# In L0's head pipeline, the product of the next gated input moves to the end of TensorE's sixth slot, and ScalarE copies it first in the seventh

## What is computed

```python
a  = tanh(einsum('ble,hde->blhd', emb, Wa_w) + Wa_b)
bg = einsum('ble,hde->blhd', emb, Wb_w) + Wb_b
h  = at * h + bt                       # scan over the tokens, for each of 8 heads
Dx = emb @ D_w.T + D_b                 # the "gated input": one for all heads
out = (einsum('blhd,hkd->blhk', hs, C_w) + C_b) * Dx[:, :, None, :]
out = _ln(out, hn_g, hn_b)
sum_heads = (Dx + einsum('h,blhd->bld', head_w, out)) / nH
z = sum_heads @ Wout_w.T + Wout_b
u = z + _ln(z, norm_g, norm_b)
ffn = gelu(u @ ffn1_w.T + ffn1_b)
return (u + (ffn @ ffn2_w.T + ffn2_b)) @ proj_w.T + proj_b
```

## Time and profile before

| | us |
|---|---|
| median of 3 runs | 1346.33 |
| lowest, highest | 1341.58, 1354.73 |
| the profiled execution | 1357.45 |
| its span | 1355.7 |
| L0's layer in it, from the first scan to the last tile's end | about 343 to 716 |

### The profile page before, as it was taken

One profiled execution on the slowest core, in us unless ns is written; L12 is line 12 of the kernel. 1 busy time (PEld: TensorE's weight loads), 2 busy tenths in 40 slices (PEclk: granted clock), 3 DMA queues, 4 the chain that ended last, 5 costly groups with the idle time before them and its releaser, 6 DMA issues.

```text
span 1355.7 us, 17322 instructions
## 1 busy us (share of the span) xinstructions
PE 1125.2 (83%) x4988; PEld 819.3 (60%) x4988; DVE 889.2 (66%) x2544; ACT 700.8 (52%) x1314; POOL 618.1 (46%) x725
## 2 busy tenths in 40 slices
PE   5866999992888999999966668999983678898996
PEld 4655877871565667666735456888861445555563
DVE  7746788773786777777727436777772377776661
ACT  4223767771456656666532214777752335554532
POOL 5864000005687888777625744000016466664440
PEclk9658999996899999999975657999995688888997
DMA  7536467751000000000000104477731000000000
GB/s 240 188 131 215 164 227 221 244 165 51 20 15 13 12 15 12 13 5 1 1 1 18 47 30 143 162 243 245 242 131 43 16 16 16 24 24 12 8 9 23
DMA packets 48958, 115.43 MB, mean 85 GB/s; under 512 B 8160, under 2 KB 14304, under 8 KB 48864
## 3 DMA queue, kind: packets, MB, share of 16 engines
q1 hardware_dynamic: 40672, 97.53, 22.0%
q0 software_dynamic: 8192, 16.79, 4.2%
HBM read 79.16 MB, written 35.13 MB: 84 GB/s over the span
## 4 chain that ended last, share of the span: by engine, by line
PE 54%; POOL 14%; DVE 12%; issue 9%; ACT 6%; another core or an unknown queue 3%; DMA 1%; SPq 0%; POOLq 0%; DVEq 0%; ACTq 0%
PE bank L188 6%; PE bank L331 4%; PE bank L333 4%; PE bank L332 4%; PE bank L345 3%; PE bank L344 3%; PE bank L343 3%; PE bank L890 2%; PE bank L1384 2%; POOL head_rstd L1101 2%; PE bank L1405 2%; PE bank L930 2%; POOL wr L488 2%; PE bank L936 2%
## 5 line engine op out<-in xcount | busy, mean ns | idle before, releaser
L609 DVE TENSOR_TENSOR hid_lo<-hid,hid_hi 128x512 fp32r<-128x512 f32 x248 | 170.3, 689 | 101.5 <-ACT hid L411 91.5
L458 POOL DMA_INDIRECT xs<-spare_all,slots x128 | 131.9, 1031 | 72.2 <-issue 37.7
L488 POOL DMA_INDIRECT got<-ys,y_slots x64 | 67.2, 1050 | 197.5 <-DMA ys<-spare_all 183.5
L411 ACT ACTIVATE hid<-bank,b_up_of 128x512 f32<-128x512 f32 x184 | 125.5, 682 | 6.2
L188 PEld LDWEIGHTS bank<-ident,spare_all 128*128 128x128 f32 x568 | 78.0, 156 | 71.6 <-issue 63.3
L410 ACT ACTIVATE hid_hi<-bank,b_up_of 128x512 fp32r<-128x512 f32 x138 | 95.0, 689 | 45.0 <-PE bank L333 34.2
L188 PE MATMUL bank<-ident,spare_all 128*128 128x128 f32 x568 | 93.9, 297 | 20.5 <-DVE spare_all L518 13.1
L984 ACT ACTIVATE gate_b<-bank,head_rstd 128x128 f32<-128x128 f32 x256 | 72.8, 369 | 49.7 <-POOL head_rstd L1101 49.5
L410 ACT ACTIVATE hid_hi<-bank,cols_sb 128x512 fp32r<-128x512 f32 x48 | 33.1, 689 | 117.4 <-PE bank L333 50.2
L331 PE MATMUL bank<-xh,wr 128*128 128x512 f32 x184 | 81.0, 440 | 0.3 <-DVE xl L602 0.2
L1555 POOL MEMSET wz<- 128x128 f32 x1 | 0.2, 204 | 175.0 <-DVEq L678 175.0
(11 more groups left out here) (284 smaller groups left out, 3114.7 us busy)
## 6 DMA issues: line engine op xcount, KB each, us to landing
wr<-wq SPq DMA_DIRECT2D x92, 512.0 KB, 4.4
spare_all<-xs SPq DMA_DIRECT2D x46, 256.0 KB, 4.8
ys<-spare_all SPq DMA_DIRECT2D x46, 256.0 KB, 5.0
wq<-wr SPq DMA_DIRECT2D x16, 512.0 KB
got<-in_w_mlp SPq DMA_DIRECT2D x9, 512.0 KB
xs<-X SPq DMA_DIRECT2D x16, 256.0 KB
xs<-spare_all,slots POOLq DMA_INDIRECT x128
out_x<-X SPq DMA_DIRECT2D x8, 256.0 KB, 2.3
```

The source lines that it names most:

```text
L411: nc.scalar.activation(hid[:, n % HC], bank[n % 3][:], ACT.Gelu_apprx_tanh, bias=bias).then_inc(s["gelu_done"], 1)
L458: g.indirect_dma_start(out=xs, out_offset=bass.IndirectOffsetOnAxis(ap=slots[:, k, n:n + 1], axis=0), in_=xn_all[:, n], in_offset=None).th ...
L488: nc.gpsimd.indirect_dma_start(out=rows_of(i, ring)[:, k, b], out_offset=None, in_=ys, in_offset=bass.IndirectOffsetOnAxis(ap=y_slots[:, k ...
L609: v.tensor_tensor(hid_lo[:, q], hid[:, n % HC], hid_hi[:, q].bitcast(F32), ALU.subtract).then_inc(s["lo_done"], 1)
```

## The change

PE's `dx_of(tile+1)` moves from between `project_head` and `c_of_head` of slot 6 to near the end of slot 5: in slot 5 it stands after `project_head`, `c_of_head`, `turn_head` and `out_of_head`. ACT's `keep_dx(tile+1)` stays in slot 6, but stands first there, ahead of `keep_head` and `share_head`; it stood behind both. Nothing is added or taken away, and all waits inside the functions stay as they are.

```diff
@@ mix_pe @@
                 if n < HEADS:
                     project_head(n)
-                if phase == DX and n // NH + 1 < TILES:
-                    dx_of(tile + 1)
                 if 0 <= n - 1 < HEADS:
                     c_of_head(n - 1)
@@
                 if phase == TURN_U and before_it is not None:
                     turn_u(before_it)
+                if phase == DX - 1 and n // NH + 1 < TILES:
+                    dx_of(tile + 1)
                 if phase == NH - 1 and before_it is not None:
                     up(before_it, 0)
@@ mix_act @@
                 tile, before_it, two_before = mix_tiles(n)
+                if phase == DX and n // NH + 1 < TILES:
+                    keep_dx(tile + 1)
                 if n < HEADS:
                     keep_head(n)
@@
                 if phase == UN and before_it is not None:
                     normalize_z(before_it)
-                if phase == DX and n // NH + 1 < TILES:
-                    keep_dx(tile + 1)
```

## The result

The changed kernel is faster. The medians of six runs each are 1328.1 us and 1350.0 us, and the ratio is 0.985 (95% interval 0.981 to 0.989). The prediction was 1332.5 us with a range of 1326 to 1341. It was counted from 1346.33 us, the median of the first three of the six runs before.

A forecast was written before the change was run, and what follows sets the result against it. PE nearly sets the pace, losing 14.5 us waiting for ACT's Dx copy. Shorter waits (9.4 us) and two thirds of 6.6 us of clock (4.4) make 13.8 us: 1346.33 to 1332.5 us, range 1326 to 1341.

The forecast's parts named there:

- The wait and its reason: Tiles 1 to 6, slot 6: PE waited 14.5 us for ACT's Dx copy, queued behind scalings awaiting POOL's root.
- The moved product: PE's next Dx product, three matmuls of 0.69 us in all, moved to slot 5: no wait added, priced at nothing.
- The moved copy: ACT's Dx copy at the front of slot 6: 0.57 us, hidden by 0.51 us of waiting for POOL.
- What ends the waits next: Slots 6 and 7: u (line 1215), then head 4's statistics (line 1167) release PE; 9.4 us gained over six tiles.
- The clock: Slot 7 of tiles 1 to 4: slow stretches of 1.64 us each go, up to 6.6 us; 4.4 us counted.
- rival 1: PE's wait goes, but slow stretches stay or turn up elsewhere: 1336.9 us, or 1340.2 at its far end; chance 0.26.
- The start: Tiles 0 and 1: PE's product could wait about 0.1 us for line 1157; put at nothing.
- The sum: Whole kernel: 9.4 us of waits and 4.4 us of clock, 13.8 us off 1346.33, giving 1332.5 us; chance 0.48.

The follow-up runs named there:

- The doubled copy: Changed kernel with one more, unread ACT copy of bank 6 at the front of slot 6: L0 306.85 us, ratio 0.990 to the kernel before.
- the filler: Kernel before with eight unused matmuls ahead of turn_u in slot 6 of tiles 1 to 6: L0 312.66 us against 319.03, ratio 0.996.
- the repetition: Changed kernel run once more, unchanged, against the kernel before: medians 1293.1 and 1307.8 us, ratio 0.989, L0 304.67 us.
- the kernel that holds PE: Changed kernel, but PE waits ahead of turn_u in tiles 1 to 6 for ACT's scalings of head 3: L0 312.35 us, ratio 0.995.
- the last kernel: Changed kernel with u normalized ahead of the scalings in tiles 1 to 5 and ACT's old order in tile 0: L0 301.42 us, ratio 0.987.

## Why the prediction was right, step by step

- **The wait and its reason.** Right. Only the copy's place behind POOL's root held PE; the copy alone moved gives the whole gain, and holding PE without touching ACT's order takes half of it back.
- **The moved product.** It was priced at nothing, and it is nothing. What the prediction did not say, though its rows held it, is that this half of the change does no work: the product was done at 497.7 with ACT free at 498.4.
- **The moved copy.** Right: 0.57 us, hidden by the 0.51 us of waiting for POOL. The doubled copy shows the price without the cover, 0.3 us a tile.
- **What ends the waits next.** Right: line 1215 and then line 1167. They were to hold PE for 0.4 us each; the view has 0.2 us of idle time for each, and by the distance of the starts (lines 890 to 188, 1.32 us instead of 0.86) the second costs the 0.4. Tile 1 is the exception, with 1.8 us of waiting for u. Per tile 1.51 and 1.88 us were worked out without the clock; tiles 5 and 6 won 1.48 and 1.85. For tiles 3 and 5 it gave 41.0 and 41.1 us, and both took 41.03.
- **The clock.** Right, and here the prediction was too careful. It took 4.4 of the 6.6 us, against rival 1. All four slow stretches went, 6.4 us by the filler. Its ground for caution, a number of slow stretches that changes from one execution to the next, is not what the two profiled executions of the kernel before show: they have them in the same four tiles. The idle times were not all equal, as it had them, either: 3.84 us in tile 1, 2.19 to 2.24 in tiles 2 to 5, 1.81 in tile 6. Between tiles 3 and 5 they were, and why only one of these fell stays open. How many slow stretches the timed runs had is not shown.
- **The start.** The term that was mis-sized. Tile 1 was counted like tiles 2 to 4, with 3.15 us, and tile 0 with nothing. Together they won 1.8. POOL is the chain there, and the copy's early end in tile 0 moved DVE's scans onto its line 1100: 1.2 us. Of the start the prediction had considered only PE's wait for line 1157, of about 0.1 us, and put it at nothing; what an earlier DVE does to POOL is no term of its sum.
- **The sum.** 13.8 us was forecast for the whole and L0 won 14.4. That they are so near is in part luck, since two errors nearly cancel: 4.4 for 6.4 us of clock, 9.4 for 8.0 us of waits. The measured 21.9 us between the medians lies further off, because the other stages differed in the same direction; the repetition has 14.7. In the time itself, 1328.1 for 1332.5 us, two more things work against each other: the median before rose from 1346.33 to 1350.0 us with three more runs, and the stages outside L0 gave about 7.5 us.

## What to carry to other kernels

When an engine waits for a copy on another engine, look at what stands ahead of the copy in that queue: if it waits for a third engine and the copy does not, moving the copy into that wait is free, up to the length of the wait. A gap on TensorE can cost most of its length again (here 1.6 us for 2.2) in matmuls at half clock behind it, which the list of waits does not show. A change of order on one engine shifts when DVE and POOL run against each other, and where POOL is the chain, a small instruction that starts inside a scan takes five times its length.

## What was not expected of the hardware

- An instruction of POOL on 128x4 elements took 1.02 to 1.16 us instead of 0.23 when it started inside DVE's scan of 128x512, and ended 0.04 us or less after it (6 of 6 in the changed kernel). The next one, line 1101, took 2.04 instead of 1.04 when it started 0.09 us into a scan (396.93 in the changed kernel). Within some hundredths of a microsecond either engine can win: with starts 0.04 us apart line 1101 took 1.04 us in the changed kernel (390.95) and 2.07 in the kernel that holds PE (375.33, line 1103 there), and in the last kernel line 1100 (1105 there) took 0.24 when it started with the scan (406.42). The other way round, a DVE instruction of 0.69 us took 1.59 when it started inside POOL's addition.
- The clock fell to the lower of its two levels (1.2 instead of 2.4 GHz) in part of slot 7 after idle times of 2.2 to 2.3 us in some tiles and not in others: in tiles 2 to 4 and not in 5, and in tiles 3 to 5 and not in 2 when only the product's place was changed. It fell behind each of the four longer ones (3.2 and 3.8 us, all in tile 1), and behind none of the waits of 1.1 to 2.0 us ahead of u's transposes. Filling the gaps with 1.84 us of unused matmuls kept it at the higher level in all six tiles.
- The length of L0 repeats to 0.1 us from one execution and one chip to another, while the stages around it scatter by 10 us. A change in one stage is better read from that stage than from the whole.
